# Layer norm's scale, shift and low part: from GpSimd to VectorE and ScalarE, in a recurrent block with a six-layer local-attention transformer

## The reference

```python
def ffn_layer(x, g, bln, W1, b1, W2, b2):
    mu = x.mean(-1, keepdims=True)
    var = ((x - mu) ** 2).mean(-1, keepdims=True)
    xn = (x - mu) / jnp.sqrt(var + 1e-05) * g + bln
    hg = xn @ W1 + b1
    a, gate = jnp.split(hg, 2, -1)
    return a * jax.nn.gelu(gate, approximate=False) @ W2 + b2
...
for i in range(DEPTH):
    x = attn_layer(shift_tokens(x), Wqkv[i], q_scale[i], k_scale[i], Wo[i]) + x
    x = ffn_layer(shift_tokens(x), ln_g[i], ln_b[i], W1[i], b1[i], W2[i], b2[i]) + x
```

## Time and profile before

| | |
|---|---|
| median of 3 runs | 3596.0 us (3595.76 to 3601.91) |
| profiled execution | 3596.09 us, span 3594.3 us |
| busy share of the span | PE 94%, DVE 88%, ACT 83%, POOL 80% |
| mean granted TensorE clock | 0.994 of full speed |

### The profile page before, as it was taken

The page is one execution under the profiler, slowest core; times in us unless marked ns, Lnnn a source line. Parts: engine busy times, 40 slices in busy tenths (PEclk is TensorE's granted clock), DMA queues, the critical chain, the costliest instruction groups (busy, mean ns, idle before and its releaser), DMA issues.

```text
span 3594.3 us, 92498 instructions
## 1 busy us (share of the span) xinstructions
PE 3394.7 (94%) x29710; PEld 2110.8 (59%) x29710; DVE 3151.4 (88%) x10872; ACT 2999.4 (83%) x8812; POOL 2877.3 (80%) x2383
## 2 busy tenths in 40 slices
PE   7887999999999999999999999999999999999998
PEld 3444656656666666666656666666666656666665
DVE  7998988988988888988988988988988988988986
ACT  6554888888888888888888888888888888888887
POOL 6887887888887888887888887888887888887883
PEclk9998999999999999999999999999999999999999
DMA  5443322333323333322333322333332333332332
GB/s 164 141 133 124 113 99 102 108 115 108 115 101 101 106 112 106 116 103 99 107 115 107 116 102 99 110 116 103 115 106 96 108 118 105 114 106 99 106 103 92
DMA packets 261726, 396.22 MB, mean 110 GB/s; under 512 B 45566, under 2 KB 86588, under 8 KB 261244
## 3 DMA queue, kind: packets, MB, share of 16 engines
q1 hardware_dynamic: 261244, 390.30, 32.4%
HBM read 157.91 MB, written 6.03 MB: 46 GB/s over the span
## 4 chain that ended last, share of the span: by engine, by line
PE 53%; DVE 17%; POOL 14%; issue 7%; ACT 6%; DMA 2%; SPq 1%; DVEq 0%; POOLq 0%; ACTq 0%
PE bank L886 9%; PE bank L875 7%; PE bank L847 6%; PE bank L360 5%; PE bank L362 5%; PE bank L361 5%; DVE ab L1610 4%; PE bank L914 4%; PE bank L829 4%; POOL rot L1359 4%; POOL pr L1345 4%; PE bank L856 4%; DVE wide L1502 3%; PE bank L857 3%; DVE sm L1655 2%
## 5 line engine op out<-in xcount | busy, mean ns | idle before, releaser
L1184 ACT ACTIVATE pr<-sm,nb,rq 128x128 f32<-128x128 f32 (+1 forms) x3072 | 1518.0, 502 | 10.8 <-DVE nb L1661 10.7
L1345 POOL TENSOR_TENSOR pr<-pr,rden 128x640 f32<-128x640 f32 x768 | 966.2, 1258 | 460.1 <-DVE rden L1635 457.7
L1359 POOL TENSOR_TENSOR rot<-ab,swp 128x512 f32<-128x512 f32 x760 | 978.0, 1287 | 74.0 <-DMA swp<-ab 73.4
L1610 DVE TENSOR_TENSOR ab<-bank,ltab 128x1024 f32<-128x1024 f32 x760 | 925.1, 1217 | 80.6 <-PE bank L362 66.7
L1655 DVE CUSTOM_DVE_ANT_0 sm<-bank,mask 128x128 f32<-128x128 f32 (+1 forms) x3072 | 839.4, 328 | 47.5 <-PE bank L847 42.1
L1184 ACT ACTIVATION_READ_ACCUMULATOR pr<-sm,nb,rq 128x1 f32 x3072 | 599.5, 195 | 0.0
L847 PEld LDWEIGHTS bank<-rot 64*64 64x64 f32 x12288 | 288.1, 132 | 436.0 <-issue 364.7
L1365 POOL TENSOR_TENSOR rot<-rot,rkb 128x512 f32<-128x512 f32 x384 | 492.3, 1289 | 64.3 <-DMA rkb<-k_scratch 64.1
L1642 DVE COPY pt<-bank 128x512 f32<-128x512 f32 x768 | 531.3, 692 | 10.2
L875 PE MATMUL bank<-pt,vtok 128*64 128x160 f32 (+1 forms) x6144 | 461.6, 292 | 29.4 <-ACT vtok L1198 29.4
L1172 ACT ACTIVATE sq<-bank 128x512 f32<-128x512 f32 x768 | 452.6, 589 | 43.2 <-DVE ab L1610 19.9
(11 more groups left out here) (213 smaller groups left out, 5743.7 us busy)
## 6 DMA issues: line engine op xcount, KB each, us to landing
swp<-ab SPq DMA_DIRECT2D x1520, 128.0 KB, 2.0
rkb<-k_scratch SPq DMA_DIRECT2D x768, 128.0 KB, 2.9
rot<-c_scratch SPq DMA_DIRECT2D x64, 256.0 KB, 3.3
sq<-c_scratch SPq DMA_DIRECT2D x64, 256.0 KB, 3.3
xs<-xT SPq DMA_DIRECT2D x95, 128.0 KB, 2.3
xs<-xT SPq DMA_DIRECT2D x95, 127.5 KB, 2.4
raw<-Wqkv SPq DMA_DIRECT2D x48, 128.0 KB, 2.7
wo<-Wo SPq DMA_DIRECT2D x6, 512.0 KB, 4.6
```

What stands on the lines that cost most here:

```text
L1184: ins = act.activation(pr[:, s % 4, i, t, 0:P + WINDOW * t], sm[:, s % 2, i, cs], ACT.Exp, bias=nb[:, s, t, i:i + 1], scale=head_scale(rq, ...
L1345: ins = pool.tensor_tensor(pr[:, e % 4, :, :, :], pr[:, e % 4, :, :, :], rden[:, e, :, :].rearrange("p t i -> p i t").unsqueeze(3) .to_bro ...
L1359: pool.tensor_tensor(rot[:, PAIRS * (j % 2) + j // 2, :], ab_of(j, 0, lead), swp_of(j, lead), ALU.add).then_inc(qk_rot, 1)
L1610: dve.tensor_tensor(ab_both(j, lead).rearrange("p i (b t) -> p i b t", b=GB), seqs(qk_bank(j, lead)[:, :]).unsqueeze(1).to_broadcast(shape ...
```

## The change

The first product of layer norm (with the inverse deviation) and the scale are done by VectorE in one instruction. The shift is left out of `xn`; ScalarE adds it as a bias when it makes `xn_h`, and VectorE adds it again when it makes `xn_l`. GpSimd does none of the three. The steps in `AT` stay. In a step, `normed` and `low` stand on VectorE behind `gated` and ahead of `clamp` and the maxima.

```diff
@@ ScalarE, turn @@
                     if s == AT["high"] and prev is not None and kind != "drain":
                         act.wait_ge(f_gb, n1 + (prev + 1))
-                        act.activation(xn_h[:, :], xn, ACT.Copy).then_inc(f_hi, 1)
+                        act.activation(xn_h[:, :], xn, ACT.Identity, bias=lv[:, V_B:V_B + 1]).then_inc(f_hi, 1)
@@ GpSimd, turn @@
-                def normed(q):
-                    ready = (n1 + (q + 1))
-                    vectors = (l + 2) if kind == "T2" else None
-                    if vectors is not None:
-                        pool.wait_ge(lv_ok, vectors)
-                    pool.wait_ge(f_xc, ready)
-                    pool.wait_ge(f_rstd, ready)
-                    pool.tensor_tensor(xn, xn, xv, ALU.mult).then_inc(f_xn, 1)
-                    pool.wait_ge(f_xn, ready)
-                    pool.tensor_scalar(xn, xn, lv[:, V_G:V_G + 1], lv[:, V_B:V_B + 1], ALU.mult, ALU.add)\
-                        .then_inc(f_gb, 1)
...
-                def low(q):
-                    pool.wait_ge(f_hi, n1 + (q + 1))
-                    pool.tensor_tensor(xn_l[:, :], xn, xn_h[:, :].bitcast(F32), ALU.subtract).then_inc(f_split, 1)
...
-                    if prev is not None and kind != "drain":
-                        if s == AT["norm"]:
-                            normed(prev)
-                        if s == AT["low"]:
-                            low(prev)
@@ VectorE, turn @@
+                def normed(q):
+                    dve.wait_ge(f_xc, n1 + (q + 1))
+                    dve.wait_ge(f_rstd, n1 + (q + 1))
+                    dve.scalar_tensor_tensor(xn, xn, lv[:, V_G:V_G + 1], xv, ALU.mult, ALU.mult).then_inc(f_gb, 1)
+
+                def low(q):
+                    dve.wait_ge(f_hi, n1 + (q + 1))
+                    dve.scalar_tensor_tensor(xn_l[:, :], xn, lv[:, V_B:V_B + 1], xn_h[:, :].bitcast(F32),
+                                             ALU.add, ALU.subtract).then_inc(f_split, 1)
...
                     for role, c in due("gated", s):
                         if group_of(role, o) is not None:
                             gated(c, group_of(role, o))
+                    if s == AT["norm"] and prev is not None and kind != "drain":
+                        normed(prev)
+                    if s == AT["low"] and prev is not None and kind != "drain":
+                        low(prev)
                     if s == AT["clamp"][1] and cur is not None:
                         clamp(1, cur)
```

More of the change, by code:

```diff
@@ L268, in build @@
         xs_in, xs2_in, cen_halves = sem("xs_in"), sem("xs2_in"), sem("cen_halves")
-        f_cen, f_xc, f_sq, f_var, f_ln, f_rstd, f_xn, f_gb, f_hi, f_split = (
-            sem(f"f_{n}") for n in ("cen", "xc", "sq", "var", "ln", "rstd", "xn", "gb", "hi", "split"))
+        f_cen, f_xc, f_sq, f_var, f_ln, f_rstd, f_gb, f_hi, f_split = (
+            sem(f"f_{n}") for n in ("cen", "xc", "sq", "var", "ln", "rstd", "gb", "hi", "split"))
         f_g, f_gelu, f_a, f_h, f_dn, f_add = (sem(f"f_{n}") for n in ("g", "gelu", "a", "h", "dn", "add"))
@@ L279, in build @@
                     p_exp, p_rden, p_norm, p_T, p_Tsb, o_ps, o_sb, at_out, at_add, f_cen, f_xc, f_sq, f_var,
-                    f_ln, f_rstd, f_xn, f_gb, f_hi, f_split, f_g, f_gelu, f_a, f_h, f_dn, f_add,
+                    f_ln, f_rstd, f_gb, f_hi, f_split, f_g, f_gelu, f_a, f_h, f_dn, f_add,
                     g_mul, g_T, g_out]
```

## The result

The changed kernel takes 3750.39 us (median of four runs, 3749.73 to 3754.45), the kernel before 3597.66 us beside it: a ratio of 1.0425, 95% interval 1.0407 to 1.0443. It is 153 us slower, on the forecast side, and 5 us above the stated range.

A forecast was written before the change was run, and what follows sets the result against it. VectorE was taken to bound step 10 to the gelu, TensorE the rest. 46 x 2.48 = 114.1 us, plus 2 for the last turn, less 14.7, gave about 3698 us; own range 3675 to 3725, 8 in 10 3655 to 3745.

The forecast's parts named there:

- Two regimes in a turn: From step 10 to the gelu VectorE sets the pace, ScalarE one step behind; from 1603.20 to 1649.00 TensorE does.
- The stall and `low`, 1.19 + 0.70: Step 11: VectorE stands 1.19 us until ScalarE's square and high part are done, then 0.70 us for `low`.
- `normed`, 0.59: Step 10: VectorE's multiply, taken as 0.70 us, makes the next `rden` 0.59 us late, 0.11 being covered.
- the third rival: VectorE and GpSimd disturb each other, both new instructions stretched to 1.25 us: +51 us, 3749 us; chance 0.07.
- TensorE's clock: Steps 12 and 13: half clock after the wait mostly covered by TensorE's slack before the gelu, a few us.
- the fourth rival: A 2.9 us TensorE wait every turn halves its clock: at most +78 us, 3776; over 20 us showing, chance 0.07.
- GpSimd's 14.7 us: All lateness beyond plain turns, over 45 turns, 14.7 us, taken as wholly regained when GpSimd's three instructions go.

The follow-up runs named there:

- the wait alone: The kernel before with nothing moved, but VectorE waiting in step 11 for the high part where the changed kernel's `low` stands: 3673.62 us, ratio 1.0213.
- The PSUM run: The changed kernel with ScalarE writing the inverse deviation into the variance's PSUM bank, so VectorE's multiply has one SBUF tensor: 3729.58 us, ratio 1.0365.
- Filling the gap: The changed kernel with TensorE doing projection 11's three passes four times instead of once in step 11: 3718.85 us, ratio 1.0336.

## Why the prediction was wrong

The direction, the mechanism and two thirds of the size were right. It said +101 us and the kernel gives +153. By its own terms:

- *Two regimes in a turn.* Right. Steps 12 and 14 are 3.46 us in the plain turn before and after, and lateness at the gelu is not made up, as the wait alone showed.
- *The stall and `low`, 1.19 + 0.70.* Right, 1.82 measured in step 11 (81.9 us over 45 turns), with 0.75 us of busy time and 0.71 for ScalarE's high part with bias (0.63 before; I had 0.09 more). Both halves of the reason, the place on VectorE and the square on ScalarE, were shown by moving each. TensorE's wait in step 12 was 2.41 us and not nearly 2.9, since the lateness of step 10 went into a wait of its own, the 0.50 us ahead of the scores of step 11.
- *`normed`, 0.59.* The first term that was mis-sized. It cost 0.98 us a turn (44.1 over 45), because the instruction lasted 1.16 us in the mean and not 0.75. That was the third rival, which I gave 0.07 and priced at both instructions: it held for one of the two, and that its 3749 us lie beside the measured 3750 is luck, as the clock made up the rest. The PSUM run removed it. I had taken the size from a row of the draining turn and from one with a PSUM operand, neither of which showed GpSimd standing in its way; that it was "at work in nearly all of these steps" stood in my own text.
- *TensorE's clock, "a few us", since "TensorE has slack before the gelu".* The second, and the larger: 35.6 us. The 2.4 us wait and what follows it do halve the clock, in 37 of the 46 full turns, the fourth rival, at 1.0 us each. The slack was looked for in the wrong place. TensorE has some before the gelu, but projection 12 has to be ready for VectorE's `products` of step 13. In the plain turn before, its last pass ran from 1594.52 to 1594.92 and `products` started at 1595.26: 0.3 us to spare, where a half-clock stretch of 3.4 us holds back 1.7 us of work. The 0.89 us wait of `products` is that, and it stands in VectorE's stretch. Filling the gap removed nearly all of it. A sign of it was in the kernel before: the turn at 1242.63, with a wait of 1.8 us and a half-clock stretch, was 2.1 us longer than a plain one, and I put all of that down to the wait; the turn behind it, from 1312.12 to 1380.74, had a wait of 2.0 us at a whole clock and was 1.2 us longer.
- *GpSimd's 14.7 us.* Right as far as can be told: the 45 turns are 161.6 us of the three terms above 45 plain turns, and nothing of the old lateness is left in them.

With the two terms at their measured size, 46 x 0.39 = 18 and 36, the sum is 101 + 54 = 155 us. Rivals that can come true beside the forecast, the clock behind its own stall and the conflict under its own multiply, are not alternatives to it, they are additions to it; the range should have held them together.

## What to carry to other kernels

In a periodic kernel, find out which engine is back to back in the very steps that an edit touches; there an instruction costs its length and a wait is paid in full, whatever the busy share over the span says. Before an instruction that waits is put ahead of others in an engine's queue, ask whether what it waits for hangs on the same engine's last output; behind them it may wait for nothing (90 us here). If a stall makes TensorE stand still, its clock and what its next matmuls release have to be priced too.

## What the runs showed of the hardware

A VectorE instruction with two SBUF tensors and a GpSimd instruction with SBUF tensors did not overlap: one stood until the other had ended, the later one where their recorded starts were over 0.03 us apart. VectorE's then took a further 0.55 us (0.74 alone). Where GpSimd's was the later, it ended 1.13 to 1.15 us behind VectorE's (1.28 alone) and took up to 1.82 us from its own start. With one of VectorE's tensors in PSUM, both kept their time (736 to 740 ns in 47 turns, and at most 1.33 us for `rotate`). The Trainium skill's page "SBUF — State Buffer" calls this an exclusive lock on a port pair that the two engines share, in which the loser waits, in its section "Who interferes with whom". The trace agrees. I had expected a stretching of both.

TensorE's clock fell to half in 37 of the 46 full turns of the changed kernel, after waits of 2.40 to 2.46 us between stretches of dense matmuls, and stayed whole in 9 with the same wait. With 1.97 to 2.13 us (the wait alone) it fell in 14 of 46, with 1.70 to 2.35 us (the high part ahead of the square) in 9, and in none with the low part behind the maxima, where no wait in the turns was longer than 1.64 us:

```profile
1347.80 0.56 PE L847 MATMUL bank<-rot 64*64 64x96 f32 x16 [1.64 <-POOL rot L1365]
```

In the kernel before, a wait of 1.8 us was followed by half the clock, and this one, one turn later, was not:

```profile
1329.68 0.56 PE L847 MATMUL bank<-rot 64*64 64x96 f32 x16 [2.00 <-POOL rot L1365]
```

Each of these stretches lasted 3.4 us. In the changed kernel that cost 1.0 us of the turn, not the 1.7 us of lost work, as some slack was there. What decides between two turns with the same wait stays open.
